# First cross attention: value tiles as the weights of the product, two heads in the array's column halves, normalised once per batch

## The chip, the cores and the metric

The kernel runs on one core of one Trainium2 chip. The time is that of one execution in device microseconds. Before the change three runs took 1884.75 to 1885.35 us, with a median of 1885.31 us; one more execution was profiled and took 1884.2 us, of which 1882.5 us are the span of its instructions. The core's engines are TensorE (PE in the profile, its weight loads PEld), VectorE (DVE), ScalarE (ACT), GpSimd (POOL) and SyncE (SP), which issues the DMAs. Each works through its own queue in order and waits on semaphores.

## What is computed

A stack of two layers. The change concerns the first step of the first layer, a cross attention with 16 batches, 64 queries per batch, 1601 keys, 16 heads of 32 columns:

```python
def _L0_xattn_ref(q, k, v, Wq, bq, Wk, bk, Wv, bv, Wo, bo):
    qh = (q @ Wq + bq).reshape(B, LQ, HEADS, D_K).transpose(0, 2, 1, 3)
    kh = (k @ Wk + bk).reshape(B, LKV, HEADS, D_K).transpose(0, 2, 1, 3)
    vh = (v @ Wv + bv).reshape(B, LKV, HEADS, D_K).transpose(0, 2, 1, 3)
    scores = jnp.einsum('bhqd,bhkd->bhqk', qh, kh) * scale
    attn = jax.nn.softmax(scores, axis=-1)
    out = jnp.einsum('bhqk,bhkd->bhqd', attn, vh)
    concat = out.transpose(0, 2, 1, 3).reshape(B, LQ, D_MODEL)
    return concat @ Wo + bo

x = x + _L0_xattn_ref(_layernorm(x), ctx_512, ctx_512, ...)   # x (16, 64, 512), ctx_512 (16, 1601, 256)
```

The rest (a state space layer, a blocked feed forward, a second cross attention, a self attention and a quantised feed forward) is as it was.

## The kernel before

`cross0` runs three blocks. `cross0_queries` makes the queries. `cross0_batches`, the one that matters here, makes the concatenated head outputs `catT`. `cross0_output` multiplies them by Wo. Float32 values are kept as two bfloat16 parts, a high part and the rest, and products are summed over the parts.

`cross0_batches` goes through 16 batches. A batch has 8 slots, one for each pair of heads (64 queries of one head in partitions 0 to 63, of the other in 64 to 127). While batch b is attended to, batch b+1's keys and values are projected. There are 29 projection groups per batch (`PROJ`): 16 for keys (six matmuls of 400 or 401 columns) and 13 for values (six of 512). `CUTS` deals them to the slots: four key groups in slots 0, 1, 3 and 5, three value groups in slots 2, 4 and 6, four value groups in slot 7. The last batch has none. The groups go through a ring of three PSUM banks.

In each slot the engines do, in the order of their queues:

- TensorE: the scores of the pair (24 matmuls in eight parts of the array, L552), the projection groups (L535), then the product of probabilities and values of the pair two slots back (L570). The scores need the exponential of the pair before (there is one buffer of scores); a group needs its ring bank free, which is when VectorE has taken the group three back.
- VectorE: the row maximum (L711), then for each group the low part (L681 or L687), for the second group of a slot the high part too (L670 or L674), and the reciprocal of the row sums (L694). In slot 2 it also takes the transposed output of the batch before, adding the bias (L722, four operations).
- ScalarE: two scalings of the product of the pair three slots back (L614, L615), the high part of the first group (L604 or L608), the exponential (L622), the high part of the third group, the high part of the probabilities (L632), the high part of the fourth group. When the exponential and L632 come is set by a count of the groups gone by: before the second and before the fourth event of the slot (the output counts as an event), or at the slot's end when there are fewer.
- GpSimd: the low part of the probabilities (L511), and the parts of the next context (L477, L484).
- SyncE: two transposing DMAs per pair (L451 high, L453 low), which bring the probabilities' parts to keys on partitions.

The product before has the transposed probabilities as weights (128 x 128) and 64 columns of values as the moving operand: high probabilities by high and low values, low probabilities by high values, 39 matmuls over 13 key tiles. Its four 32-column blocks hold two useful ones (each head's queries by its own values). L614 and L615 take these two into `o`, scaled by the reciprocal row sums. In slot 2 TensorE transposes `o` (L579, two transposes).

Of the kernel before, what the change touches and what calls it, by code (L numbers as in the profile page):

```python
# [314 lines left out]
EXP_AFTER = 1  # L315
NPT = len(PTILES)
# [44 lines left out]
def cross0_batches(k, ident, qT, wk, wv, bk, catT, bvT, wo):  # L361
    nc, d = k.nc, k.d
    with ExitStack() as ctx:
# [5 lines left out]
        v = k.sb(ctx, "x0_v", [P, 2, 2, NPT, D], BF16)  # L369
# [5 lines left out]
        rsum = k.sb(ctx, "x0_rowsum", [P, 4])  # L375
        rinv = k.sb(ctx, "x0_rowinv", [P, 4])
        o = spare[:, 2 * NKT:2 * NKT + 2 * NPAIR * DH].rearrange("p (u a d) -> p u a d", u=2, a=NPAIR)
# [25 lines left out]
        o_done = k.sem(ctx, "x0_o_done")  # L403
        wo_in = k.sem(ctx, "x0_wo_in")
        s_cat = k.sem(ctx, "x0_cat_done")
# [109 lines left out]
        def _(pe):  # L515
# [69 lines left out]
            for b, plan in enumerate(PLANS):  # L585
                for p in range(len(plan)):
                    if b < B:
                        scores_of(b, p)
                    for e, g, _ in ring_events(b, p):
# [4 lines left out]
                        else:  # L594
                            turned_out(e[1], g)

        @block.scalar
        def _(act):
            def project_hi(n, par, g):
# [18 lines left out]
            def exps(g):
                act.wait_ge(max_done, g + 1)
                if g >= 2:  # L620
# [3 lines left out]
                                     accum_out=rsum[:, g % 4:g % 4 + 1]).then_inc(exp_done, 1)  # L624
# [11 lines left out]
            for b, plan in enumerate(PLANS):  # L636
                for p in range(len(plan)):
                    pair = NPAIR * b + p
                    if 3 <= pair:
                        scaled(pair - 3)  # L640
                    todo = [exps, high] if b < B else []
                    seen = 0
                    for e, g, vector in ring_events(b, p):
# [7 lines left out]
                        if vector or e[0] == "out":  # L651
# [3 lines left out]
                    for do in todo:  # L655
                        do(pair)

        @block.vector
        def _(dve):
# [5 lines left out]
            def project_hi(n, par, g):  # L665
# [1667 lines left out]
```

## Time and profile before

| | us |
|---|---|
| median of three runs | 1885.31 |
| profiled execution | 1884.2 |
| its span | 1882.5 |

Of the span TensorE is busy 1635.2 us (87%), VectorE 1167.6 (62%), ScalarE 961.3 (51%), GpSimd 772.1 (41%). The first cross attention's batches run from about 100 to 895 us. In the page's row of slices TensorE shows 9 tenths or more there and the granted clock is full until the last batch. A timeline line gives start, duration, engine, source line, operation, output <- inputs, shape, count, and in brackets the idle time before it with what ended it. A matmul's duration in the list reaches past the start of the next one, so the pace is read from start to start. A slot is read from one row maximum on VectorE to the next. Some matmul records are missing, so a count can be short.

### The profile page before, as it was taken

To read this page: it belongs to the slowest core of one execution; us is meant where nothing else is said; L and a number is where in the kernel's file an instruction comes from. 1 tells how busy PE (TensorE), PEld (TensorE's weight loads), DVE (VectorE), ACT (ScalarE), POOL (GpSimd) and SP (SyncE) were. 2 spreads that over 40 slices of the span, in tenths; PEclk is the share of its full clock that TensorE was granted. 3 is DMA by queue.
4 is the path that set the end of the run, shared out by engine and by line. 5 is a ranking of instruction groups with operands and counts; after the bars stand their busy time and mean duration, and the time that the engine had idled before them with its cause. 6 is when DMAs were issued, how large, how long until landed. Compare 5 with 4: busy or idle time off the path is not lost. (4 is left out here: it accounts for less than half of the span.)

```text
span 1882.5 us, 36647 instructions
## 1 busy us (share of the span) xinstructions
PE 1635.2 (87%) x15032; PEld 888.8 (47%) x15144; DVE 1167.6 (62%) x1931; ACT 961.3 (51%) x1444; POOL 772.1 (41%) x379
## 2 busy tenths in 40 slices
PE   4799999999999999996889828989889989699449
PEld 2345555555555555554445413445434444344214
DVE  4477777877777787773555586779512221626891
ACT  1268888888888888875162323421102221227760
POOL 2257877777777787765000163532000000002410
PEclk9899999999999999995999868999999999799769
DMA  3459999999999999998300140234647944000001
GB/s 109 119 123 183 186 186 184 183 187 186 187 189 187 184 191 184 184 164 149 113 1 2 52 156 29 80 110 136 245 167 304 388 180 177 1 1 1 0 0 45
DMA packets 509506, 256.62 MB, mean 136 GB/s; under 512 B 443040, under 2 KB 490656, under 8 KB 506400
## 3 DMA queue, kind: packets, MB, share of 16 engines
q1 hardware_dynamic: 509344, 254.34, 58.4%
q8 instruction: 116, 1.90, 0.4%
q14 instruction: 46, 0.38, 0.1%
HBM read 130.29 MB, written 14.16 MB: 77 GB/s over the span
## 5 line engine op out<-in xcount | busy, mean ns | idle before, releaser
L511 POOL TENSOR_TENSOR x<-x_prob,x 128x1604 bf16<-128x1604 f32 x128 | 413.3, 3229 | 181.2 <-ACT x L632 180.9
L622 ACT ACTIVATE x_prob<-x_score,x_negmax 128x1604 f32<-128x1604 f32 x128 | 204.4, 1597 | 75.7 <-DVE x_negmax L711 74.7
L711 DVE TENSOR_REDUCE x_negmax<-x_score 128x1 f32<-128x1604 f32 x128 | 231.9, 1812 | 13.1 <-PE x_score L552 13.1
L681 DVE SCALAR_TENSOR_TENSOR x_kT<-x_ring,bk,x_kT 128x400 bf16<-128x400 f32 (+1 forms) x256 | 162.5, 635 | 118.3 <-ACT x_kT L604 115.6
L535 PE MATMUL x_ring<-x_ctx_hi,wk_split 128*128 128x400 bf16 (+1 forms) x1024 | 218.6, 335 | 11.6 <-POOL x_ctx_lo L484 9.3
L535 PE MATMUL x_ring<-wv_split,x_ctx_hi 128*128 128x512 bf16 (+1 forms) x770 | 200.3, 379 | 9.7 <-issue 9.6
L632 ACT CAST x<-x_prob 128x1604 bf16<-128x1604 f32 x128 | 195.9, 1531 | 0.3
L570 PEld LDWEIGHTS x_pv<-x_v,x_pT 128*128 128x128 bf16 (+1 forms) x4992 | 170.4, 100 | 42.5 <-ACT x L615 10.8
L570 PE MATMUL x_pv<-x_v,x_pT 128*128 128x64 bf16 (+1 forms) x4992 | 176.2, 196 | 14.0 <-DMA x_pT<-x 7.8
L687 DVE TENSOR_TENSOR x_v<-x_ring,x_v 128x512 bf16<-128x512 f32 (+1 forms) x208 | 143.2, 688 | 53.6 <-ACT x_v L608 51.5
L604 ACT ACTIVATE x_kT<-x_ring,bk 128x400 bf16<-128x400 f32 (+1 forms) x196 | 116.8, 596 | 76.8 <-PE x_ring L535 76.3
L535 PEld LDWEIGHTS x_ring<-x_ctx_hi,wk_split 128*128 128x128 bf16 x1024 | 92.1, 97 | 105.5 <-issue 16.5
L2009 PE MATMUL g_bank<-g_x_split,g_w 128*128 128x512 bf16 x564 | 126.1, 384 | 8.6 <-DVE g_x_split L2108 8.0
L535 PE MATMUL x_ring<-x_ctx_lo,wk_split 128*128 128x400 bf16 (+1 forms) x512 | 129.4, 334 | 0.0
L535 PEld LDWEIGHTS x_ring<-wv_split,x_ctx_hi 128*128 128x128 bf16 (+1 forms) x832 | 77.4, 99 | 102.3 <-issue 14.4
L535 PE MATMUL x_ring<-wv_split,x_ctx_lo 128*128 128x512 bf16 (+1 forms) x415 | 123.5, 379 | 0.1
L1975 POOL MEMSET g_round<- 128x1 f32 x1 | 0.1, 98 | 289.1 <-POOLq L1672 289.1
L484 POOL TENSOR_TENSOR x_ctx_lo<-x_stage,x_ctx_hi 128x802 bf16<-128x802 f32 (+1 forms) x64 | 106.4, 1663 | 15.9 <-DVE x_ctx_hi L663 14.6
L608 ACT CAST x_v<-x_ring 128x512 bf16<-128x512 f32 (+1 forms) x148 | 86.1, 582 | 52.3 <-PE x_ring L535 52.3
L2019 PE MATMUL g_bank<-g_wd,g_w 128*128 128x512 bf16 x282 | 63.6, 386 | 52.8 <-DVE g_w L2192 52.4
L1219 PE MATMUL f_bank<-f_x_split,f_w 128*128 128x512 bf16 x374 | 90.9, 392 | 12.7 <-POOL f_w L1106 12.1
L552 PE MATMUL x_score<-x_kT,x_q_rows 32*64 32x400 bf16 (+1 forms) x3072 | 94.7, 345 | 6.0 <-ACT x_prob L622 6.0
(313 smaller groups left out, 2539.2 us busy)
## 6 DMA issues: line engine op xcount, KB each, us to landing
y_ctx<-in_ctx SPq DMA_DIRECT2D x16, 1664.0 KB, 10.4
y_ctxT<-in_ctxT SPq DMA_DIRECT2D x16, 1601.0 KB, 14.0
x_stage<-in_ctxT SPq DMA_DIRECT2D x48, 400.0 KB, 4.5
x_q_rows<-q_rows SPq DMA_DIRECT2D x64, 128.0 KB, 3.3
f_split_stage<-in_L_ffn_w SPq DMA_DIRECT2D x8, 1024.0 KB, 5.2
x_stage<-in_ctxT SPq DMA_DIRECT2D x16, 401.0 KB, 4.8
x_pT<-x SPq DMA_TRANSPOSE x256, 4.5
f_split_stage<-in_L_ffn_w_up SPq DMA_DIRECT2D x12, 256.0 KB, 3.0
```

Source lines behind the costliest of these rows:

```text
L484: pool.tensor_tensor(clo[:, :, at], stage[:, c % 2, :, 0:n], chi[:, :, at], ALU.subtract).then_inc(clo_done, 1)
L511: pool.tensor_tensor(ph[:, g % 2, 1, 0:NKP], prob[:, g % 2, :], ph[:, g % 2, 0, 0:NKP], ALU.subtract).then_inc(pl_done, 1)
L535: last = pe.matmul(out_, lhs, rhs, start=(i == 0), stop=(i == len(steps) - 1))
L552: last = pe.matmul(score[L * u:L * u + L, 512 * c:512 * c + w], qp[rows, par, a, hq, p // 2, :], kT[rows, par, hk, p // 2, QW * c:QW * c + w],
L570: last = pe.matmul(pv[:, 0:2 * DH], pT[0:kw, u, hp, t, :], v[0:kw, vpar, hv, t, 2 * DH * pp:2 * DH * (pp + 1)], start=(hp == 0 and t == 0 ...
L604: nc.scalar.activation(kT[:, par, 0, m, n0:n0 + w], ring[g % RING][:, 0:w], ACT.Identity, bias=bk[:, KD * turned(c) + m:KD * turned(c) + m ...
L622: nc.scalar.activation(prob[:, g % 2, :].rearrange("p (c n) -> p c n", n=QW), scores, ACT.Exp, bias=nmax[:, g % 2:g % 2 + 1], accum_out=rs ...
L632: nc.scalar.copy(ph[:, g % 2, 0, 0:NKP], prob[:, g % 2, :]).then_inc(ph_done, 1)
L681: dve.scalar_tensor_tensor(kT[:, par, 1, m, n0:n0 + w], ring[g % RING][:, 0:w], bk[:, KD * turned(c) + m:KD * turned(c) + m + 1], kT[:, pa ...
L687: dve.tensor_tensor(v[0:kw, par, 1, m, :], ring[g % RING][0:kw, :], v[0:kw, par, 0, m, :], ALU.subtract).then_inc(ring_free, 1)
L711: dve.tensor_reduce(nmax[:, pair % 2:pair % 2 + 1], scores, mybir.AxisListType.XY, ALU.max, negate=True).then_inc(max_done, 1)
L2009: last = pe.matmul(banks[2 + n % NB_G][:], wt[:, hw, j, m * P:(m + 1) * P], xs[:, hx, j, 512 * c:512 * c + 512], start=(i == 0 and j == 0) ...
```

## The change

The operands of the product change places. The values are stored by head with the high and the low part beside one another (`v`, 64 columns for each head), and these 64 columns are the weights. The moving operand is 128 columns: 64 queries' high and 64 low probabilities of one head. The first head of a pair writes partitions 0 to 63 of the bank, the second 64 to 127, each in its half of the array's columns. That is 26 matmuls over the 13 key tiles. The result has rows (value part, value column) and columns (probability part, query), so both the columns' halves and the rows' halves must be added. VectorE adds the columns' halves for each pair (`summed`, a reduction of 128 values into 64, in place of ScalarE's two scalings). The rows' halves are added once per batch on TensorE (`folded`, replacing the two transposes): two float32 products with a folding matrix, and sixteen that spread the reciprocal row sums over the rows of the output. Then ScalarE copies these shares from PSUM (in slot 2's place of the output), VectorE multiplies the folded sums by them into `catT`, and ScalarE adds the bias at the head of slot 3 (`biased`, four operations). The product now waits for both transposes before its first matmul, and for `sum_done` in place of `o_done`.

```diff
@@ products @@
                 if g:
-                    pe.wait_ge(o_done, g)
+                    pe.wait_ge(sum_done, g)
                 pe.wait_ge(th_in[u], 16 * (g // 2 + 1))
-                for hp in range(2):
-                    if hp:
-                        pe.wait_ge(tl_in[u], 16 * (g // 2 + 1))
-                    for t, (k0, kw) in enumerate(PTILES):
-                        for hv in range(2 - hp):
-                            last = pe.matmul(pv[:, 0:2 * DH], pT[0:kw, u, hp, t, :],
-                                             v[0:kw, vpar, hv, t, 2 * DH * pp:2 * DH * (pp + 1)],
-                                             start=(hp == 0 and t == 0 and hv == 0), stop=(hp == 1 and t == NPT - 1))
+                pe.wait_ge(tl_in[u], 16 * (g // 2 + 1))
+                for t, (k0, kw) in enumerate(PTILES):
+                    for h in range(2):
+                        last = pe.matmul(pv[L * h:L * h + L, 0:2 * L],
+                                         v[0:kw, vpar, t, 2 * pp + h, :, :].rearrange("p s d -> p (s d)"),
+                                         pT[0:kw, u, :, t, L * h:L * h + L], start=(t == 0), stop=(t == NPT - 1))
                 last.then_inc(pv_done, 1)
 
-            def turned_out(b, g):
-                pe.wait_ge(o_done, NPAIR * (b + 1))
+            def folded(b, g):
+                if b == 0:
+                    pe.wait_ge(fold_set, 1)
+                pe.wait_ge(sum_done, NPAIR * (b + 1))
                 wait_bank(g)
-                for h in range(2):
-                    last = pe.transpose(ring[g % RING][:, P * h:P * h + P],
-                                        o[:, b % 2, 4 * h:4 * h + 4, :].rearrange("p a d -> p (a d)"), ident[:])
+                pe.wait_ge(inv_done, NPAIR * (b + 1))
+                for r in range(2):
+                    pe.matmul(ring[g % RING][L * r:L * r + L, 0:4 * L], fold[:].rearrange("p h d -> p (h d)"),
+                              sums[:, r::2, :], start=True, stop=True)
+                for n in range(4):
+                    for r in range(2):
+                        for h in range(2):
+                            pair = (NPAIR * b + 2 * n + r) % NINV
+                            rows = slice(L * r + DH * h, L * r + DH * h + DH)
+                            last = pe.matmul(ring[g % RING][rows, 4 * L + L * n:4 * L + L * n + L],
+                                             rinv[:, pair:pair + 1].broadcast_to([P, DH]), ident[:, L * h:L * h + L],
+                                             start=True, stop=True)
                 last.then_inc(ring_full, 1)
@@ ScalarE @@
-            def scaled(g):
-                pp, opar = g % NPAIR, g // NPAIR % 2
-                act.wait_ge(inv_done, g + 1)
-                act.wait_ge(pv_done, g + 1)
-                nc.scalar.activation(o[0:L, opar, pp, :], pv[0:L, 0:DH], ACT.Copy, scale=rinv[0:L, g % 4:g % 4 + 1])
-                nc.scalar.activation(o[L:P, opar, pp, :], pv[L:P, DH:2 * DH], ACT.Copy,
-                                     scale=rinv[L:P, g % 4:g % 4 + 1]).then_inc(o_done, 1)
+            def biased(b, g):
+                act.wait_ge(ring_free, g + 1)
+                for n in range(4):
+                    tile = catT[:, n, L * b:L * b + L]
+                    nc.scalar.activation(tile, tile, ACT.Identity, bias=bvT[:, n:n + 1])
...
-                    if 3 <= pair:
-                        scaled(pair - 3)
+                    while shifted:
+                        biased(*shifted.pop())
...
-                        if vector or e[0] == "out":
+                        if e[0] == "out":
+                            act.wait_ge(hi_done, g)
+                            act.wait_ge(ring_full, g + 1)
+                            nc.scalar.copy(shares, ring[g % RING][:, 4 * L:8 * L]).then_inc(hi_done, 1)
+                            shifted.append((e[1], g))
+                            continue
+                        if vector:
                             continue
@@ VectorE @@
             def inverse(g):
                 dve.wait_ge(exp_done, g + 1)
-                if g >= 4:
-                    dve.wait_ge(o_done, g - 3)
-                dve.reciprocal(rinv[:, g % 4:g % 4 + 1], rsum[:, g % 4:g % 4 + 1]).then_inc(inv_done, 1)
+                dve.reciprocal(rinv[:, g % NINV:g % NINV + 1], rsum[:, g % NINV:g % NINV + 1]).then_inc(inv_done, 1)
+
+            def summed(g):
+                dve.wait_ge(pv_done, g + 1)
+                dve.tensor_reduce(sums[:, g % NPAIR, :], pv[:, 0:2 * L].rearrange("p (s q) -> p q s", s=2), AX,
+                                  ALU.add).then_inc(sum_done, 1)
...
                         dve.tensor_reduce(nmax[:, pair % 2:pair % 2 + 1], scores, mybir.AxisListType.XY, ALU.max,
                                           negate=True).then_inc(max_done, 1)
+                    if 3 <= pair:
+                        summed(pair - 3)
...
                         elif e[0] == "out":
-                            dve.wait_ge(ring_full, g + 1)
-                            tok = slice(L * e[1], L * e[1] + L)
-                            for n in range(4):
-                                dve.tensor_scalar(catT[:, n // 2, n % 2, tok], ring[g % RING][:, L * n:L * n + L],
-                                                  bvT[:, n:n + 1], None, ALU.add).then_inc((hi_done, s_cat, s_cat, ring_free)[n], 1)
+                            dve.wait_ge(hi_done, g + 1)
+                            dve.tensor_tensor(catT[:, :, L * e[1]:L * e[1] + L],
+                                              ring[g % RING][:, 0:4 * L].rearrange("p (n q) -> p n q", n=4),
+                                              shares.rearrange("p (n q) -> p n q", n=4), ALU.mult).then_inc(ring_free, 1)
```

The tables `rsum` and `rinv` grow from 4 to 16 columns, the layouts of `v`, `catT`, the bias and Wo follow, and the writers of `v` write 32 columns at a time with a gap.

The order of the queues around the output. First ScalarE in a steady batch, slot 2 of batch 1 and the head of slot 3, before (x_prob is the probabilities, x their high part or, for L614 and L615, `o`):

```order
L608 CAST x_v<-x_ring 128x512
L622 ACTIVATE x_prob,x_rowsum<-x_score,x_negmax 128x1604
L608 CAST x_v<-x_ring 128x512
L632 CAST x<-x_prob 128x1604
L614 ACTIVATE x<-x_pv,x_rowinv 64x32
L615 ACTIVATE x<-x_pv,x_rowinv 64x32
L604 ACTIVATE x_kT<-x_ring,bk 128x400
```

and now (L667 is the copy of the shares, L635 the bias):

```order
L620 CAST x_v<-x_ring 128x16x32
L627 ACTIVATE x_prob,x_rowsum<-x_score,x_negmax 128x1604
L620 CAST x_v<-x_ring 128x16x32
L645 CAST x<-x_prob 128x1604
L667 COPY x<-x_ring 128x256
L635 ACTIVATE catT<-catT,bvT 128x64 x4
L616 ACTIVATE x_kT<-x_ring,bk 128x400
```

The copy stands behind the high part of the probabilities (L645), and the bias ahead of the next slot's first group. In the last batch there are no groups, and ScalarE's queue there now reads, slots 1 to 4:

```order
L627 ACTIVATE x_prob,x_rowsum<-x_score,x_negmax 128x1604
L645 CAST x<-x_prob 128x1604
L667 COPY x<-x_ring 128x256
L627 ACTIVATE x_prob,x_rowsum<-x_score,x_negmax 128x1604
L645 CAST x<-x_prob 128x1604
L635 ACTIVATE catT<-catT,bvT 128x64 x4
L627 ACTIVATE x_prob,x_rowsum<-x_score,x_negmax 128x1604
L645 CAST x<-x_prob 128x1604
L627 ACTIVATE x_prob,x_rowsum<-x_score,x_negmax 128x1604
```

Here the copy stands ahead of the slot's exponential. On TensorE the end of slot 2 of batch 1 reads now:

```order
L538 MATMUL x_ring<-wv_split,x_ctx_hi 128x512 x4
L538 MATMUL x_ring<-wv_split,x_ctx_lo 128x512 x2
L571 MATMUL x_pv<-x_pT,x_v 64x128 x26
L583 MATMUL x_ring<-x,x_fold 64x256 x2
L590 MATMUL x_ring<-ident,x_rowinv 32x64 x16
L555 MATMUL x_score<-x_kT,x_q_rows 64x401 x2
L555 MATMUL x_score<-x_kT,x_q_rows 64x400 x6
```

Eighteen matmuls stand where two transposes (L579) stood, between the product and the next scores.

## Rows read from the trace of the kernel before

**Rows 1.** Busy time by engine, 300 to 400 us (busy, instructions; clock, DMA, GB/s).

```profile
300.00:400.00 100.00, 98.60 (x1364) 58.74 (x1371) 78.51 (x118) 81.35 (x126) 78.71 (x34) 1.00 1.02 184
```

**Rows 2.** Timeline of DVE, one batch: start, us, operation, count [idle before, releaser].

```profile
395.24 1.83 DVE L711 TENSOR_REDUCE x_negmax<-x_score 128x1 f32<-128x1604 f32 x1 [0.32 <-PE x_score L552]
...
402.45 1.80 DVE L711 TENSOR_REDUCE x_negmax<-x_score 128x1 f32<-128x1604 f32 x1
...
409.04 1.81 DVE L711 TENSOR_REDUCE x_negmax<-x_score 128x1 f32<-128x1604 f32 x1
...
415.62 1.81 DVE L711 TENSOR_REDUCE x_negmax<-x_score 128x1 f32<-128x1604 f32 x1
...
419.66 0.69 DVE L687 TENSOR_TENSOR x_v<-x_ring,x_v 128x512 bf16<-128x512 f32 x1 [0.31 <-ACT x_v L608]
420.27 0.85 DVE L722 TENSOR_SCALAR catT<-x_ring,bvT 128x64 f32<-128x64 f32 x4
...
421.11 1.81 DVE L711 TENSOR_REDUCE x_negmax<-x_score 128x1 f32<-128x1604 f32 x1
...
427.69 1.81 DVE L711 TENSOR_REDUCE x_negmax<-x_score 128x1 f32<-128x1604 f32 x1
...
432.40 1.81 DVE L711 TENSOR_REDUCE x_negmax<-x_score 128x1 f32<-128x1604 f32 x1
...
438.99 1.81 DVE L711 TENSOR_REDUCE x_negmax<-x_score 128x1 f32<-128x1604 f32 x1
...
444.11 1.83 DVE L711 TENSOR_REDUCE x_negmax<-x_score 128x1 f32<-128x1604 f32 x1 [0.31 <-PE x_score L552]
```

**Rows 3.** Timeline of ACT, the same batch.

```profile
399.25 0.58 ACT L608 CAST x_v<-x_ring 128x512 bf16<-128x512 f32 x1 [0.29 <-PE x_ring L535]
...
404.29 1.60 ACT L622 ACTIVATE x_prob<-x_score,x_negmax 128x1604 f32<-128x1604 f32 x1 [0.23 <-DVE x_negmax L711]
...
406.36 1.52 ACT L632 CAST x<-x_prob 128x1604 bf16<-128x1604 f32 x1
407.78 0.60 ACT L604 ACTIVATE x_kT<-x_ring,bk 128x401 bf16<-128x401 f32 x1
```

**Rows 4.** Timeline of PE, the same batch.

```profile
399.00 1.03 PE L535 MATMUL x_ring<-wv_split,x_ctx_hi 128*68 128x512 bf16 x4
...
402.18 0.85 PE L535 MATMUL x_ring<-x_ctx_hi,wk_split 128*128 128x401 bf16 x4
...
406.27 1.31 PE L570 MATMUL x_pv<-x_v,x_pT 128*128 128x64 bf16 x39
407.50 0.72 PE L552 MATMUL x_score<-x_kT,x_q_rows 32*64 32x401 bf16 x24
408.15 0.85 PE L535 MATMUL x_ring<-x_ctx_hi,wk_split 128*128 128x400 bf16 x4
...
419.41 0.41 PE L579 MATMUL x_ring<-ident,x 128*128 128x128 f32 x2
```

**Rows 5.** Timeline of PE, later stages: products in column parts, float32 (two records each).

```profile
976.49 0.43 PE L940 MATMUL m_banks<-m_mix,m_xn 128*32 128x128 f32 x8 [1.79 <-DVE m_mix L1056]
...
1416.75 1.95 PE L1576 MATMUL y_pv<-y_ctx,y_pT 128*64 128x256 f32 x16 [0.24 <-ACT y_pT L1614]
...
1555.52 7.05 PE L1718 MATMUL s_bank<-s_xT,s_wq 128*64 128x512 f32 x16 [0.77 <-ACT s_xT L163]
```

**Rows 6.** Groups by shape, ACT, 90 to 900 us: busy and mean ns of one.

```profile
L608 ACT CAST x_v<-x_ring 128x512 bf16<-128x512 f32 x129 | 75.0, 582 | 49.5 <-PE x_ring L535 49.4
L615 ACT ACTIVATE x<-x_pv,x_rowinv 64x32 f32<-64x32 f32 x128 | 36.1, 282 | 1.6
```

**Rows 7.** Timeline of DVE, last batch.

```profile
847.17 1.83 DVE L711 TENSOR_REDUCE x_negmax<-x_score 128x1 f32<-128x1604 f32 x1 [1.16 <-PE x_score L552]
...
852.08 1.83 DVE L711 TENSOR_REDUCE x_negmax<-x_score 128x1 f32<-128x1604 f32 x1 [1.16 <-PE x_score L552]
...
877.95 1.83 DVE L711 TENSOR_REDUCE x_negmax<-x_score 128x1 f32<-128x1604 f32 x1 [1.53 <-PE x_score L552]
...
892.58 0.86 DVE L722 TENSOR_SCALAR catT<-x_ring,bvT 128x64 f32<-128x64 f32 x4 [10.89 <-PE x_ring L579]
```

**Rows 8.** Busy time by engine, 850 to 900 us (as rows 1).

```profile
850.00:900.00 50.00, 32.56 (x475) 22.00 (x473) 13.73 (x21) 25.94 (x39) 23.27 (x8) 0.60 0.88 166
```

**Rows 9.** Timeline of SP's queue, last transposing load.

```profile
886.39 1.48 SPq L453 DMA_TRANSPOSE x_pT<-x  x1
```

**Rows 10.** Timeline of PE, end of the stage.

```profile
890.25 0.88 PE L570 MATMUL x_pv<-x_v,x_pT 128*128 128x64 bf16 x13 [1.57 <-DMA x_pT<-x]
```

**Rows 11.** DMA issues of the page: operation, count, us to landing.

```profile
x_pT<-x SPq DMA_TRANSPOSE x256, 4.5
```

More of the change, by code:

```diff
@@ L315 @@
 EXP_AFTER = 1
+NINV = 16
 NPT = len(PTILES)
@@ L374, in cross0_batches @@
         nmax = k.sb(ctx, "x0_negmax", [P, 2])
-        rsum = k.sb(ctx, "x0_rowsum", [P, 4])
-        rinv = k.sb(ctx, "x0_rowinv", [P, 4])
-        o = spare[:, 2 * NKT:2 * NKT + 2 * NPAIR * DH].rearrange("p (u a d) -> p u a d", u=2, a=NPAIR)
+        rsum = k.sb(ctx, "x0_rowsum", [P, NINV])
+        rinv = k.sb(ctx, "x0_rowinv", [P, NINV])
+        sums = spare[:, 2 * NKT:2 * NKT + NPAIR * L].rearrange("p (a q) -> p a q", a=NPAIR)
+        shares = spare[:, 2 * NKT + NPAIR * L:2 * NKT + NPAIR * L + 4 * L]
+        fold = k.sb(ctx, "x0_fold", [P, 2, DH])
         zero = k.sb(ctx, "x0_zero", [P, KC])
@@ L402, in cross0_batches @@
         inv_done = k.sem(ctx, "x0_inv_done")
-        o_done = k.sem(ctx, "x0_o_done")
+        sum_done = k.sem(ctx, "x0_sum_done")
+        fold_set = k.sem(ctx, "x0_fold_set")
         wo_in = k.sem(ctx, "x0_wo_in")
-        s_cat = k.sem(ctx, "x0_cat_done")
         block = ctx.enter_context(nc.Block())
@@ L594, in _ @@
                         else:
-                            turned_out(e[1], g)
+                            folded(e[1], g)
         @block.scalar
@@ L607, in project_hi @@
                     kw = PTILES[m][1]
-                    nc.scalar.copy(v[0:kw, par, 0, m, :], ring[g % RING][0:kw, :]).then_inc(hi_done, 1)
-            def scaled(g):
-                pp, opar = g % NPAIR, g // NPAIR % 2
-                act.wait_ge(inv_done, g + 1)
-                act.wait_ge(pv_done, g + 1)
-                nc.scalar.activation(o[0:L, opar, pp, :], pv[0:L, 0:DH], ACT.Copy, scale=rinv[0:L, g % 4:g % 4 + 1])
-                nc.scalar.activation(o[L:P, opar, pp, :], pv[L:P, DH:2 * DH], ACT.Copy,
-                                     scale=rinv[L:P, g % 4:g % 4 + 1]).then_inc(o_done, 1)
+                    nc.scalar.copy(v[0:kw, par, m, :, 0, :],
+                                   ring[g % RING][0:kw, :].rearrange("p (h d) -> p h d", h=H)).then_inc(hi_done, 1)
             def exps(g):
@@ L656, in _ @@
                         do(pair)
+            biased(*shifted.pop())
         @block.vector
@@ L673, in project_hi @@
                     kw = PTILES[m][1]
-                    dve.tensor_copy(v[0:kw, par, 0, m, :], ring[g % RING][0:kw, :]).then_inc(hi_done, 1)
+                    dve.tensor_copy(v[0:kw, par, m, :, 0, :],
+                                    ring[g % RING][0:kw, :].rearrange("p (h d) -> p h d", h=H)).then_inc(hi_done, 1)
             def project_lo(n, par, g):
@@ L686, in project_lo @@
                     kw = PTILES[m][1]
-                    dve.tensor_tensor(v[0:kw, par, 1, m, :], ring[g % RING][0:kw, :], v[0:kw, par, 0, m, :],
-                                      ALU.subtract).then_inc(ring_free, 1)
+                    dve.tensor_tensor(v[0:kw, par, m, :, 1, :],
+                                      ring[g % RING][0:kw, :].rearrange("p (h d) -> p h d", h=H),
+                                      v[0:kw, par, m, :, 0, :], ALU.subtract).then_inc(ring_free, 1)
             def inverse(g):
                 dve.wait_ge(exp_done, g + 1)
-                if g >= 4:
-                    dve.wait_ge(o_done, g - 3)
-                dve.reciprocal(rinv[:, g % 4:g % 4 + 1], rsum[:, g % 4:g % 4 + 1]).then_inc(inv_done, 1)
+                dve.reciprocal(rinv[:, g % NINV:g % NINV + 1], rsum[:, g % NINV:g % NINV + 1]).then_inc(inv_done, 1)
[3 more added lines that the diff above has]
+                                  ALU.add).then_inc(sum_done, 1)
+            half = ident[:].rearrange("p (h s d) -> p h s d", h=2, s=2)
+            dve.tensor_tensor(fold[:], half[:, :, 0, :], half[:, :, 1, :], ALU.add).then_inc(fold_set, 1)
             for c in range(1, 4):
@@ L758, in _ @@
                 for i in range(4):
-                    last = pe.matmul(banks[t % NB_O][:], catT[:, i // 2, i % 2, t * P:(t + 1) * P], wo[:, i, :],
+                    last = pe.matmul(banks[t % NB_O][:], catT[:, i, t * P:(t + 1) * P], wo[:, i, :],
                                      start=(i == 0), stop=(i == 3))
@@ L2203, in cross0 @@
     with ExitStack() as c0:
-        catT = k.sb(c0, "catT", [P, 2, 2, TOK])
+        catT = k.sb(c0, "catT", [P, 4, TOK])
         bvT = k.sb(c0, "bvT", [P, 4])
@@ L2283, in lay_out @@
     f = np.ascontiguousarray
-    pairs = lambda a: a.reshape((2, 4, 2, DH) + a.shape[1:])
     ctx = i["ctx_512"]
@@ L2292, in lay_out @@
         "L0_xattn_bq": columns(i["L0_xattn_bq"]), "L0_xattn_bk": f(np.concatenate([np.roll(columns(i["L0_xattn_bk"]), ROWS * g, axis=0) for g in range(NROW)], axis=1)),
-        "L0_xattn_bv": f(pairs(i["L0_xattn_bv"]).transpose(1, 3, 0, 2).reshape(P, 4)),
-        "L0_xattn_Wo": f(pairs(i["L0_xattn_Wo"]).transpose(0, 2, 1, 3, 4).reshape(4, P, D)),
+        "L0_xattn_bv": columns(i["L0_xattn_bv"]),
+        "L0_xattn_Wo": f(i["L0_xattn_Wo"].reshape(4, P, D)),
         "L0_xattn_bo": f(i["L0_xattn_bo"].reshape(1, D)),
```

5 lines of the change are left out of this document (3 added, 2 removed).

## The prediction

> **What bounds the kernel now.** I read first the busy shares of the first cross attention, which fills about 100 to 895 us of the profiled execution. In its steady part TensorE is busy 98.6% at the full granted clock, ScalarE 81%, VectorE 79%, GpSimd 79% [rows 1]. By that view alone TensorE is the bound and every microsecond taken from it is won. The second view, the timeline of VectorE, says something else. Each slot (one pair of heads) begins on VectorE with the row maximum, so the starts of these reductions are the slots' lengths [rows 2]: 7.21 us for slot 7 of a batch (four value groups), 6.58 for each of the four slots with four key groups (402.45 to 409.04 to 415.62, 421.11 to 427.69, 432.40 to 438.99), 5.49 for slot 2 (three value groups and the output of the last batch), 4.71 for slot 4 and 5.12 for slot 6 (three value groups). A batch is 48.87 us (395.24 to 444.11). Only slot 7's reduction carries an idle time that ends with TensorE's scores, 0.32 us in one batch and 0.31 in the next. The others start because VectorE itself is through.
>
> ScalarE's timeline shows why [rows 3]. With R the start of the maximum, the exponential starts at R+1.84, the high part of the probabilities at R+3.91, the fourth group's high part at R+5.33, and VectorE's low part of that group and the reciprocal bring the next R at 6.58. Nothing of this key slot is TensorE's. A three-group slot closes already behind the third group, at 4.71. A four-value slot would need about 6.61 in the same way. So this chain of ScalarE and VectorE asks 4 x 6.58 + 2 x 4.71 + 5.49 + 6.61 = 47.8 us a batch.
>
> TensorE asks about as much [rows 4]: four key groups 4.09 us (402.18 to 406.27), so 1.02 each and 0.425 ns a column; a value group 1.02 x 512/401 = 1.30; the product with the values 1.23 (406.27 to 407.50); the scores 0.65 (407.50 to 408.15); the two transposes about 0.35 of the 0.41 shown. A batch: 16 x 1.02 + 13 x 1.30 + 8 x 1.88 + 0.35 = 48.6. The two chains are bound alternately, and what TensorE costs beyond the other one is 48.87 - 47.8 = 1.0 us a batch: 0.60 in slot 7, 0.41 in slot 6. That is all that a cheaper TensorE can win.
>
> **The change, TensorE.** Removed are 39 products of 64 columns (1.23 us). Added are 26 of 128 columns in alternating column halves. If halves overlap fully, 13 x 128 x 0.425 = 0.71 us; if not at all, 1.41. Later stages run float32 products in the same form, 128 rows and 64 columns [rows 5]: eight of 256 columns, alternating between the halves, take 1.95 us, 0.95 ns a column, while eight of 512 columns in one half take 7.05, 1.72 ns a column. Halves do overlap. I take 0.85, and keep 0.71 to 1.41. The fold adds two float32 products of 256 columns in two halves (0.49 by the first of these rates) and sixteen of 64 columns, 32 wide, in four column quarters. Four of that width and 128 columns took 0.43 [rows 5], so at most 4 x 0.43 = 1.7; streaming alone would be 0.4. I take 1.7 for the fold, keep 0.9 to 2.6 (all of them one behind the other, 1,536 columns at 1.72 ns). The new sum: 33.2 + 8 x (0.65 + 0.85) + 1.7 = 46.9 us a batch, below the other chain.
>
> The page "TensorE: Matmul & The Clock Gate" of the Trainium skill, section Back-to-back issue gap, gives about 81 ns for each matmul of 128 columns in a sustained stream with its weight load. That would be 2.1 us for the 26 products, more than is removed. "TensorEngine Tiling (Array Packing)" of the Trainium skill, Gotcha 2, adds that column tiling excludes the fast weight load. The trace has no bfloat16 pair of this shape; its float32 one overlaps, which is why I do not follow these rules for the forecast.
>
> **The change, VectorE.** Each slot gets one reduction of 128 values per row behind the maximum. The maximum reads 1604 in 1.81; small operations of 64 columns cost 0.21 each (four in 0.85), so I take 0.25, within 0.2 to 0.35. It lies where VectorE waits for ScalarE later in the slot: 0.31 us before the last low part of a three-group slot [rows 2], more in the others. It costs nothing up to 0.31, and 0.04 in three slots at 0.35.
>
> **The change, ScalarE.** The two scalings leave (0.28 us each [rows 6]). They stand at the head of a slot, where ScalarE has slack before the maximum ends, so they return nothing. In slot 2 there is a new step on the chain. Now VectorE reaches the output right after the third low part. In the changed order ScalarE does the third high part, then the 1.52 us high copy of the probabilities, and only then copies the 128 x 256 shares out of PSUM; VectorE multiplies after that. ScalarE is free at R+5.33. The copy is between 0.28 (32 columns) and 0.58 (512) [rows 6], I take 0.43; the multiplication 0.42 (0.69 for 512 less 256 at 1.04 ns); 0.03 more for reciprocal and hand-overs. Slot 2 becomes 6.20 instead of 5.49: +0.71. The fold must be full by R+5.33: the groups end near R+2.4, the product at 3.25, the fold at 4.95, and 0.25 later the reader starts (the group ended 399.00, ScalarE took it at 399.25). It just fits; a fold of 2.6 us would add 0.8. In slot 3 four bias operations, 0.3 each, come before the first high part; they end near R+1.2, that part takes 0.5 of ScalarE, and the exponential is still due at R+1.84. They are hidden by 0.1 us.
>
> **The steady sum.** Slot 6 returns to 4.71: -0.41. In slot 7 TensorE starts its scores only after the exponential of slot 6 (R+3.6), is through with three value groups at slot 7's R+3.4, and ScalarE can take the third at R+3.66 instead of R+3.43: the slot is 6.84, -0.37. With +0.71 in slot 2: -0.07 a batch. Fourteen batches give -1.0; the first batch has no output: -0.8. Together -1.8 us, with -8 (copy and multiplication at their least, slot 7 whole) to +12 (fold at 2.6) around it.
>
> **The end of the stage.** In the last batch no projections cover anything. Nominal slots are 4.91 [rows 7], the five to 877.95 average 5.17, and the clock's mean is 0.60 [rows 8]: the lower level, 1.2 GHz, most of the time. Here I count the new product as 1.5 us and the fold as 2.6.
> - In slot 2 the shares' copy now stands ahead of the exponential in ScalarE's queue, because no group pulls the exponential forward. The low transpose is issued at R+8.44 (877.95 to 886.39 [rows 7, 9]) and lands 3.9 (890.25, [rows 10]) to 4.5 us later [rows 11]. So the product of two slots back starts at R+2.5 to 3, ends near 4.2, the fold near 6.8, the copy near 7.3: the exponential starts some 5.3 us after R+1.84, and all of the chain behind it. About 1.3 us of present waits for transposes are absorbed.
> - The product now waits for both transposes before its first instruction: of today's 0.88 us after the last landing [rows 10] it makes 1.5. Where the transpose is last, three slots carry 0.6 more: 0.2 a slot, 1.2 in six.
> - After the last landing today 3.2 us remain (890.25 to 892.58 + 0.86 [rows 7, 10]). New: 1.5 + 0.25 + 2.6 + 0.43 + 0.42 + four bias operations 1.1 + hand-overs 0.3 = 6.6: +3.4 (at full clock 5.1, +1.9).
>
> Sum: 5.3 - 1.3 + 1.2 + 3.4 = +8.6 us, within 4 and 12. With the steady part: 8.6 - 1.8 = +6.8. The profiled execution was 1884.2 us (span 1882.5); its median of three 1885.3. Forecast: 1891.0 on the profiled one, 1892.1 for the median.
>
> **Rivals.**
> - *Small end.* The last batch overlaps more than I count (full clock, fold 1.3 us): +4 there, -4 in the steady part. 1885.5, no change. For it: both parts have such lower ends. Against: the queue order of ScalarE in the last batch is fixed.
> - *TensorE is the bound after all.* For it: 98.6% busy. Then a batch follows its sum, 46.9 instead of 48.87, 15 x -2.0 = -29.5, +8.6 at the end: 1864. It decides if key slots fall below 6.58. Against: four slots a batch show no wait for TensorE. It also holds, in a weaker form (down to about 1880), if slots 2 and 7 come shorter.
> - *Halves do not overlap in bfloat16* (weight loads of 64 columns in the open). Product 1.41, fold 2.6: 33.2 + 5.2 + 11.3 + 2.6 = 52.3 a batch, +3.4 x 15 = 51, with the end about 1945. It decides from a product of 1.05 us. (By the 81 ns of the Trainium skill's page above the product would be 2.1 us and the time near 2030.)
>
> **Chances.** Forecast 0.64, small end 0.16, TensorE bound 0.12, no overlap 0.08. The range 1884 to 1903 leaves the last two out; the forecast's own is 1888 to 1898. About 0.2%, 3.8 us, is what a measurement here tells from no change. Faster by more 0.12, within 0.17, slower 0.71.
>
> **What the next profile would show.** Product groups start to start 0.8 to 0.9; TensorE's steady busy share down by one or two points with waits on the exponential and on ring banks; key slots still 6.58; slot 2 near 6.2 with the shares' copy behind the high copy; slot 6 at 4.71; one slot of 10 us in the last batch. I am wrong if key slots change, if the product is above 1.05, or if the batch is not 48.8.

## The result and the profile after

The changed kernel takes 1890.38 us in the median of 14 runs, against 1885.09 us of the kernel before in the same session: a ratio of 1.0025, 95% interval 1.0014 to 1.0037. It is slower by 0.25%, 5.3 us. Its profiled execution has a span of 1889.2 us, 6.7 more than before. The last operation on `catT` ends at 900.23 us instead of 893.44, 6.8 later, and what follows takes 989.0 us in both profiles. So in these two executions all of the difference lies in this stage.

Busy time of the changed kernel, a steady stretch and the last batch (busy us and instructions of PE, PEld, DVE, ACT, POOL; granted clock, DMA share, GB/s):

```profile
300.00:400.00 100.00, 96.33 (x1246) 51.31 (x1252) 80.04 (x126) 76.81 (x105) 78.85 (x35) 1.00 1.01 184
850.00:900.00 50.00, 23.13 (x424) 15.08 (x400) 14.86 (x23) 22.72 (x29) 22.55 (x7) 0.52 0.72 129
```

TensorE has fallen from 98.6% to 96.3% and ScalarE from 81 to 77 [rows 1]. Both got work taken away, and a batch got only 0.06 us shorter.

VectorE's timeline, one batch (start, duration, operation; the row maxima are the slots, L718 is the sum of the columns' halves, L749 the multiplication by the shares):

```profile
394.37 1.81 DVE L738 TENSOR_REDUCE x_negmax<-x_score 128x1 f32<-128x1604 f32 x1
...
401.24 1.80 DVE L738 TENSOR_REDUCE x_negmax<-x_score 128x1 f32<-128x1604 f32 x1
...
409.56 0.28 DVE L718 TENSOR_REDUCE x<-x_pv 128x64 f32<-128x128 f32 x1
...
414.42 1.81 DVE L738 TENSOR_REDUCE x_negmax<-x_score 128x1 f32<-128x1604 f32 x1
...
420.16 0.42 DVE L749 TENSOR_TENSOR catT<-x_ring,x 128x256 f32<-128x256 f32 x1 [1.01 <-ACT x L667]
...
420.57 1.81 DVE L738 TENSOR_REDUCE x_negmax<-x_score 128x1 f32<-128x1604 f32 x1
...
438.46 1.81 DVE L738 TENSOR_REDUCE x_negmax<-x_score 128x1 f32<-128x1604 f32 x1
...
443.18 1.81 DVE L738 TENSOR_REDUCE x_negmax<-x_score 128x1 f32<-128x1604 f32 x1
```

Slot by slot against [rows 2], the maxima left out included: slot 7 6.87 (7.21 before), the two key slots 6.59 and 6.59, slot 2 6.15 (5.49), slot 3 6.59, slot 4 4.72, slot 5 6.58, slot 6 4.72 (5.12). A batch is 48.81 us (48.87). The sum of the halves takes 0.28 us and 0.19 to 0.20 of VectorE's row, and no slot is longer for it.

TensorE, slots 0 to 2 of the next batch (L571 the product, L583 and L590 the fold, L555 the scores, L538 a group):

```profile
404.97 0.92 PE L571 MATMUL x_pv<-x_pT,x_v 128*64 128x128 bf16 x26
405.82 0.71 PE L555 MATMUL x_score<-x_kT,x_q_rows 32*64 32x401 bf16 x24
...
410.44 0.85 PE L538 MATMUL x_ring<-x_ctx_hi,wk_split 128*128 128x400 bf16 x4 [0.74 <-DVE x_kT L702]
...
417.80 0.60 PE L583 MATMUL x_ring<-x,x_fold 128*64 128x256 f32 x4
418.33 0.65 PE L590 MATMUL x_ring<-ident,x_rowinv 128*32 128x64 f32 x32
418.92 0.72 PE L555 MATMUL x_score<-x_kT,x_q_rows 32*64 32x401 bf16 x24
```

The product takes 0.85 us from start to start (404.97 to 405.82; 1.23 before) and the fold 1.12 (417.80 to 418.92). The saving turns into a wait: at 410.44 the fourth key group stands 0.74 us idle until VectorE frees its bank.

ScalarE around the output, slot 2 and the head of slot 3:

```profile
418.32 1.54 ACT L645 CAST x<-x_prob 128x1604 bf16<-128x1604 f32 x1
419.75 0.38 ACT L667 COPY x<-x_ring 128x256 f32<-128x256 f32 x1
420.62 1.07 ACT L635 ACTIVATE catT<-catT,bvT 128x64 f32<-128x64 f32 x4 [0.49 <-DVE catT L749]
...
422.42 1.60 ACT L627 ACTIVATE x_prob<-x_score,x_negmax 128x1604 f32<-128x1604 f32 x1 [0.25 <-DVE x_negmax L738]
```

The copy of the shares (0.38 us) starts at 419.75, right behind the high copy, while the fold had been ready since 418.92. VectorE had stood idle for 1.01 us until this copy let it multiply, at 420.16. The four bias operations end before the exponential is due, which still waits 0.25 us for the maximum.

The last batch on TensorE:

```profile
854.69 1.60 PE L571 MATMUL x_pv<-x_pT,x_v 128*64 128x128 bf16 x26 [4.00 <-DMA x_pT<-x]
856.05 1.09 PE L583 MATMUL x_ring<-x,x_fold 128*64 128x256 f32 x4
...
896.24 1.12 PE L583 MATMUL x_ring<-x,x_fold 128*64 128x256 f32 x4 [0.38 <-DVE x L718]
```

On ScalarE, in the last batch:

```profile
858.28 0.37 ACT L667 COPY x<-x_ring 128x256 f32<-128x256 f32 x1 [7.30 <-PE x_ring L590]
858.55 1.60 ACT L627 ACTIVATE x_prob<-x_score,x_negmax 128x1604 f32<-128x1604 f32 x1
...
899.17 1.06 ACT L635 ACTIVATE catT<-catT,bvT 128x64 f32<-128x64 f32 x4 [0.49 <-DVE catT L749]
```

On VectorE, in the last batch:

```profile
850.78 1.83 DVE L738 TENSOR_REDUCE x_negmax<-x_score 128x1 f32<-128x1604 f32 x1 [1.17 <-PE x_score L555]
...
861.60 1.83 DVE L738 TENSOR_REDUCE x_negmax<-x_score 128x1 f32<-128x1604 f32 x1 [1.16 <-PE x_score L555]
...
881.90 1.83 DVE L738 TENSOR_REDUCE x_negmax<-x_score 128x1 f32<-128x1604 f32 x1 [1.17 <-PE x_score L555]
```

One slot is 10.82 us (850.78 to 861.60): the product waits for its transposing load until 854.69, the fold follows at the lower clock (1.2 GHz: the mean granted clock is 0.50 from 850 to 862), ScalarE stands idle for 7.30 us until the fold lets it copy, and only then comes the exponential (858.55, R+7.77). The last row maximum stands at 881.90 instead of 877.95 [rows 7].

### The profile page after: what moved, and what is told of

Same layout as the page of the kernel before. It is cut to its first block and busy times, and to the rows that moved or that the text cites. A ratio compares the mean times of both kernels' runs of the same rounds, so it can differ in the third digit from the quotient of the medians.

```text
span 1889.2 us, 34092 instructions
## 1 busy us (share of the span) xinstructions
PE 1613.7 (85%) x13912; PEld 826.2 (44%) x14024; DVE 1182.6 (63%) x2012; ACT 922.8 (49%) x1268; POOL 773.2 (41%) x379
## 3 DMA queue, kind: packets, MB, share of 16 engines
q1 hardware_dynamic: 509344, 254.34, 56.9%
## 5 line engine op out<-in xcount | busy, mean ns | idle before, releaser
L538 PE MATMUL x_ring<-x_ctx_hi,wk_split 128*128 128x400 bf16 (+1 forms) x1024 | 218.5, 335 | 27.7 <-DVE x_kT L702 18.4
L538 PE MATMUL x_ring<-wv_split,x_ctx_hi 128*128 128x512 bf16 (+1 forms) x770 | 200.3, 379 | 9.7 <-issue 9.4
L645 ACT CAST x<-x_prob 128x1604 bf16<-128x1604 f32 x128 | 195.9, 1531 | 0.3
L571 PE MATMUL x_pv<-x_pT,x_v 128*64 128x128 bf16 (+1 forms) x3328 | 124.3, 228 | 27.7 <-DMA x_pT<-x 16.5
L538 PEld LDWEIGHTS x_ring<-x_ctx_hi,wk_split 128*128 128x128 bf16 x1024 | 89.6, 97 | 127.7 <-DVE x_kT L702 39.9
L571 PEld LDWEIGHTS x_pv<-x_pT,x_v 128*64 128x64 bf16 (+1 forms) x3328 | 102.7, 114 | 77.9 <-issue 50.7
L538 PE MATMUL x_ring<-x_ctx_lo,wk_split 128*128 128x400 bf16 (+1 forms) x512 | 129.2, 334 | 0.0
L538 PE MATMUL x_ring<-wv_split,x_ctx_lo 128*128 128x512 bf16 (+1 forms) x415 | 123.5, 379 | 0.1
L538 PEld LDWEIGHTS x_ring<-wv_split,x_ctx_hi 128*128 128x128 bf16 (+1 forms) x832 | 77.3, 99 | 102.3 <-issue 14.7
L487 POOL TENSOR_TENSOR x_ctx_lo<-x_stage,x_ctx_hi 128x802 bf16<-128x802 f32 (+1 forms) x64 | 106.4, 1664 | 16.7 <-DVE x_ctx_hi L683 15.4
L1247 PE MATMUL f_bank<-f_x_split,f_w 128*128 128x512 bf16 x374 | 91.1, 393 | 13.3 <-POOL f_w L1134 12.8
L555 PE MATMUL x_score<-x_kT,x_q_rows 32*64 32x400 bf16 (+1 forms) x3072 | 95.2, 347 | 4.9 <-ACT x_prob L627 3.8
```

Of the source, the lines that this page charges most:

```text
L487: pool.tensor_tensor(clo[:, :, at], stage[:, c % 2, :, 0:n], chi[:, :, at], ALU.subtract).then_inc(clo_done, 1)
L538: last = pe.matmul(out_, lhs, rhs, start=(i == 0), stop=(i == len(steps) - 1))
L571: last = pe.matmul(pv[L * h:L * h + L, 0:2 * L], v[0:kw, vpar, t, 2 * pp + h, :, :].rearrange("p s d -> p (s d)"), pT[0:kw, u, :, t, L * h ...
L645: nc.scalar.copy(ph[:, g % 2, 0, 0:NKP], prob[:, g % 2, :]).then_inc(ph_done, 1)
```

## The experiments

The medians, and three lengths from the profiles, in us (the kernel before ran beside them, with medians of 1885.9 beside e1 to e4 and 1886.0 beside e5 to e8). "Stage" is the time from the first row maximum to the end of the last operation on `catT`, "last batch" the part of it from the last batch's first row maximum on. The batch is the mean of the fourteen that have an output:

| kernel | median | ratio to before, 95% | stage | a batch, mean | last batch |
|---|---|---|---|---|---|
| before | 1885.1 | | 784.3 | 48.87 | 51.2 |
| changed | 1890.4 | 1.0014 to 1.0037 | 791.1 | 48.84 | 59.3 |
| e1 | 1870.7 | 0.9907 to 0.9946 | 772.3 | 48.16 | 50.0 |
| e2 | 1878.9 | 0.9945 to 0.9981 | 778.1 | 48.57 | 51.3 |
| e3 | 1876.6 | 0.9932 to 0.9969 | 777.1 | 48.06 | 59.0 |
| e4 | 1888.9 | 1.0002 to 1.0029 | 787.7 | 48.83 | 56.0 |
| e5 | 1876.5 | 0.9925 to 0.9962 | 774.2 | 48.00 | 56.9 |
| e6 | 1893.8 | 1.0032 to 1.0075 | 791.4 | 48.93 | 58.3 |
| e7 | 1934.0 | 1.0225 to 1.0266 | 832.4 | 51.31 | 64.0 |
| e8 | 1861.6 | 0.9848 to 0.9887 | 761.4 | 47.13 | 56.4 |

The stage is counted from its first row maximum because its start differs: it stands at 109.1 us in the profiles of before and changed and at 106.5 to 108.6 in those of e1 to e8, behind code that no edit touches. Ends of the stage can therefore not be compared across these profiles.

**e1: how much the product can give at all.**

```diff
-                    for t, (k0, kw) in enumerate(PTILES):
+                    for t, (k0, kw) in enumerate(PTILES[0:1]):
...
-                                             start=(hp == 0 and t == 0 and hv == 0), stop=(hp == 1 and t == NPT - 1))
+                                             start=(hp == 0 and t == 0 and hv == 0), stop=(hp == 1 and t == 0))
```

> The kernel before with its product of probabilities and values summed over one key tile of thirteen (3 matmuls instead of 39), so most of the product is left out. Theory (ScalarE and VectorE hold a batch at 47.8 us whatever TensorE does): slot 6 falls from 5.12 to 4.7, slot 7 from 7.21 to 6.6, the key slots stay at 6.58 and slot 2 at 5.5; a batch 47.8 instead of 48.87, 15 of them -16 us, and the last batch -2 more: about 1867. Rival (TensorE is the bound): the whole product comes back, about 1.15 us x 8 x 15 = -138 us, about 1747.

Busy time of e1, the steady stretch:

```profile
300.00:400.00 100.00, 84.61 (x818) 42.18 (x824) 79.72 (x119) 82.25 (x126) 80.17 (x34) 1.00 0.96 189
```

VectorE of e1, slots 0 and 7 and the starts behind them:

```profile
395.26 1.80 DVE L711 TENSOR_REDUCE x_negmax<-x_score 128x1 f32<-128x1604 f32 x1
...
401.84 1.81 DVE L711 TENSOR_REDUCE x_negmax<-x_score 128x1 f32<-128x1604 f32 x1
...
436.53 1.81 DVE L711 TENSOR_REDUCE x_negmax<-x_score 128x1 f32<-128x1604 f32 x1
...
443.40 1.80 DVE L711 TENSOR_REDUCE x_negmax<-x_score 128x1 f32<-128x1604 f32 x1
```

This kernel leaves 36 of the product's 39 matmuls out, so its output is not the attention. That takes TensorE from 98.6 to 84.6% busy and saves 15 us, not 138 (12.0 of them in the stage). Key slots are 6.58 and 6.59, slot 2 is 5.48. The rival is refuted. One size of the theory was off: slot 7 is 6.87 (436.53 to 443.40), as in the changed kernel, as its four value groups after late scores make it, by the sum in the prediction; a batch is 48.14, not 47.8. So the most that a cheaper TensorE could win was 0.73 us a batch, and not the 1.0 of the prediction.

**e2 and e3: the chain of ScalarE and VectorE shortened, before and after the change.** The same two lines go from both kernels:

```diff
-                        elif seen == EXP_AFTER + 2 and todo:
-                            todo.pop(0)(pair)
```

> The kernel before with ScalarE's high copy of the probabilities moved behind the fourth group's high part. Theory: the chain of ScalarE and VectorE shrinks in the four key slots and slot 7 from 6.58 to about 5.2, but TensorE then asks 48.6 us a batch, so only 0.3 a batch comes back: -4 us, about 1881, key slots near 6.0 and TensorE without idle time. Rival (only the ScalarE and VectorE chain counts): -1.4 x 5 x 15 = -100 us.

> The changed kernel with the same move. Theory: here TensorE asks only 47.0 us a batch (key slots 5.67, slots of three value groups 5.49, slot 2 6.51, slot 7 6.79), so a batch falls from 48.80 to 47.0 to 47.3: -22 to -27 us against the changed kernel, about 1865, and the same edit is worth some 20 us more here than in the kernel before. Rival (TensorE's saving is lost elsewhere, on the transposing loads or GpSimd): a batch stays above 48 and TensorE waits for x_pT; -5 us or less.

VectorE of e2, the first row maximum of a batch and that of the next:

```profile
396.41 1.83 DVE L709 TENSOR_REDUCE x_negmax<-x_score 128x1 f32<-128x1604 f32 x1 [0.40 <-PE x_score L552]
...
444.99 1.83 DVE L709 TENSOR_REDUCE x_negmax<-x_score 128x1 f32<-128x1604 f32 x1 [0.40 <-PE x_score L552]
```

In e2 nearly every maximum now waits 0.4 us for the scores, a batch is 48.58 us, which is TensorE's sum (48.6), and the time falls by 7 us where 4 were expected. The stage is 6.2 us shorter: 4.2 in the fourteen batches with an output, as expected, and 2.2 in the first batch, which the sum had left out; the last one is not shorter. In e3 the key slots are 5.68 as TensorE's sum has them, but the time fell by 14 us against the changed kernel, not by 22 to 27. The direction is right, the size was not, and the rival named beside it came in part: the mean batch stays at 48.06 instead of 47.0 to 47.3. ScalarE of e3, slot 2 and the head of slot 3:

```profile
411.21 0.37 ACT L665 COPY x<-x_ring 128x256 f32<-128x256 f32 x1 [1.31 <-PE x_ring L590]
411.48 1.53 ACT L645 CAST x<-x_prob 128x1604 bf16<-128x1604 f32 x1
...
414.35 1.59 ACT L627 ACTIVATE x_prob<-x_score,x_negmax 128x1604 f32<-128x1604 f32 x1
```

The copy waits 1.31 us for the fold, with the high copy (411.48), the bias and the next exponential (414.35) queued behind it: slots 2 and 3 are 6.72 and 5.91 instead of 6.51 and 5.67, 6.3 us in fourteen batches. A second loss is in slots 5 and 6, which are up to 1.6 us too long in some batches, 8.4 us in all. TensorE's waits of e3 for these loads, 150 to 820 us (us in total, times, longest):

```profile
PE x_pv L571 <- DMA x_pT<-x: 7.6, 12, 1.5
```

And the same of the changed kernel:

```profile
PE x_pv L571 <- DMA x_pT<-x: 0.5, 1, 0.5
```

The transposing loads are now sometimes last.

**e4 and e5: the last batch.** In e4, in the last batch alone, ScalarE does exponential and high copy ahead of the copy of the shares; e5 is e3 with this:

```diff
                         if e[0] == "out":
+                            while b == B - 1 and todo:
+                                todo.pop(0)(pair)
                             act.wait_ge(hi_done, g)
```

> The changed kernel; in the last batch alone ScalarE does exponential and high copy before the copy of the shares. Theory: the slot of 10.82 us falls to 8.3, not to 5, because VectorE's multiplication by the shares still stands ahead of the next row maximum in its queue (copy at R+7.5, multiplication to R+8.3): -2.5 us, about 1888. Rival (the queue order of ScalarE is all of it): slot at 5.2, -5.5 us.

> The changed kernel with the high copy behind the fourth group's high part and, in the last batch alone, exponential and high copy ahead of the copy of the shares. The two gains lie in different places: -14 us and -2 to -3 against the changed kernel, about 1873. Rival (the last batch hides one of them): 1876.

The slot of the output in e4, two lines of TensorE and two of VectorE:

```profile
850.88 1.60 PE L571 MATMUL x_pv<-x_pT,x_v 128*64 128x128 bf16 x26 [2.79 <-DMA x_pT<-x]
...
854.28 1.23 PE L555 MATMUL x_score<-x_kT,x_q_rows 32*64 32x401 bf16 x24
...
854.88 0.42 DVE L751 TENSOR_TENSOR catT<-x_ring,x 128x256 f32<-128x256 f32 x1 [4.68 <-ACT x L669]
...
855.58 1.83 DVE L740 TENSOR_REDUCE x_negmax<-x_score 128x1 f32<-128x1604 f32 x1 [0.21 <-PE x_score L555]
```

The slot that began at 848.17 is 7.41 us instead of 10.82, between the 8.3 of the theory and the 5.2 of the rival. The theory's reason is not what the rows show: behind VectorE's multiplication (854.88) the row maximum still waits 0.21 us for the scores, and these stand in TensorE's queue behind the fold and a product that waited 2.79 us for its load. So it is the late load and the fold on TensorE that keep this slot long. The last batch is 3.2 us shorter than in the changed kernel. The median fell by only 1.5, and e5's not at all against e3 (its last batch is 2.1 us shorter). These are sizes that the medians do not resolve: e4's profiled execution had a span of 1896.0 us with 1001.6 of it after the stage, 12.6 more than the changed kernel's, in code that is the same. So the gain is shown for the last batch, not for the whole time.

**e6: the copy before the high copy, nothing else.**

```diff
-                        elif seen == EXP_AFTER + 2 and todo:
+                        elif seen == EXP_AFTER + 2 and todo and e[0] != "out":
```

> The changed kernel with one step moved: in the output's slot the copy of the shares stands ahead of the high copy, all else in the old order. Theory: VectorE is through with the slot at R+5.5 instead of 6.15, but ScalarE then still has 1.4 us of high copy, 1.1 of bias and 0.5 of a group before the next exponential, which starts at R+8.05 as against 7.99 now: what slot 2 gives, slot 3 takes, 0 to +1 us. Rival (the place of the copy on the chain is what the change loses): -0.65 x 14 = -9 us.

ScalarE of e6, slot 2 and the next slot's exponential:

```profile
418.17 0.37 ACT L667 COPY x<-x_ring 128x256 f32<-128x256 f32 x1 [0.69 <-PE x_ring L590]
418.44 1.53 ACT L645 CAST x<-x_prob 128x1604 bf16<-128x1604 f32 x1
...
421.31 1.59 ACT L627 ACTIVATE x_prob<-x_score,x_negmax 128x1604 f32<-128x1604 f32 x1
```

Slot 2 is 5.51 and slot 3 7.05, together 12.56 against 12.74: as said, slot 3 takes what slot 2 gives, and the rival's 9 us did not come. Slots 6 and 7 are longer in some batches, where TensorE waited for late transposing loads (eight times, 4.1 us in all, from 150 to 820 us; once, 0.5 us, in the changed kernel). The time is 3.4 us above the changed kernel's, where 0 to 1 was expected. The stage is only 0.3 us longer, so where the rest of these 3.4 us lies is open; the two intervals overlap.

**e7: one column half at a time.**

```diff
-                for t, (k0, kw) in enumerate(PTILES):
-                    for h in range(2):
+                for h in range(2):
+                    for t, (k0, kw) in enumerate(PTILES):
```

> The changed kernel with the product's loops exchanged: all 13 tiles of the first head in one column half, then all 13 of the second, same matmuls and weights. Theory (the halves overlap in time, which makes the 26 products 0.85 us): without it 26 x 54.4 ns = 1.41 us or a little more, TensorE asks 47.0 + 8 x 0.56 = 51.5 us a batch and becomes the bound: +2.7 x 15 = +40 us, and some +4 in the last batch at the lower clock, about 1935. Rival (the 0.85 us come from fewer weight loads, not from overlap): start to start stays 0.85 us and the time 1890.

TensorE of e7, one product and the scores behind it:

```profile
419.19 1.45 PE L571 MATMUL x_pv<-x_pT,x_v 128*64 128x128 bf16 x26
420.57 0.71 PE L555 MATMUL x_score<-x_kT,x_q_rows 32*64 32x401 bf16 x24
```

The same 26 matmuls take 1.38 us (419.19 to 420.57), a batch 51.3, and the time is 1934.0. With the same matmuls and weights, only the alternation differs: so the halves do overlap in the changed kernel, and the order of two loops is worth 44 us.

**e8: the version that beats both.** e3, and at the output, in every batch, what is left to do for the pair comes first:

```diff
                         if e[0] == "out":
+                            while todo:
+                                todo.pop(0)(pair)
                             act.wait_ge(hi_done, g)
```

> As the one before it, but in every batch the high copy of the output's slot stands ahead of the copy of the shares. Theory: with the copy first, ScalarE idles for the fold and does the high copy late, which makes slots 2 and 3 of 6.72 and 5.91 us where TensorE asks 6.51 and 5.67; with the high copy first both fall to that, -0.45 x 14 = -6 us: about 1867. Rival (the copy then stands late again, as in the changed kernel, R+6.15, and VectorE's next slot with it): slot 3 gets longer by what slot 2 gets shorter, 1873.

Busy time of e8, the steady stretch:

```profile
300.00:400.00 100.00, 98.22 (x1285) 53.77 (x1293) 85.96 (x133) 80.22 (x106) 81.35 (x35) 1.00 1.05 194
```

VectorE of e8, slots 2 and 3, and slot 2 of the next batch:

```profile
399.31 1.83 DVE L738 TENSOR_REDUCE x_negmax<-x_score 128x1 f32<-128x1604 f32 x1
...
406.06 1.81 DVE L738 TENSOR_REDUCE x_negmax<-x_score 128x1 f32<-128x1604 f32 x1
...
411.49 1.83 DVE L738 TENSOR_REDUCE x_negmax<-x_score 128x1 f32<-128x1604 f32 x1
...
446.29 1.83 DVE L738 TENSOR_REDUCE x_negmax<-x_score 128x1 f32<-128x1604 f32 x1
```

Its waits for the transposing loads, 150 to 820 us:

```profile
PE x_pv L571 <- DMA x_pT<-x: 1.1, 4, 0.4
```

Slots 2 and 3 are 6.75 and 5.43, 12.18 together, which is TensorE's 6.51 + 5.67. This batch (399.31 to 446.29) is 46.98 us, TensorE's sum again (the mean is 47.13), and the waits for transposing loads fell from 7.6 to 1.1 us. 1861.6 us is 0.9868 of the kernel before (0.9848 to 0.9887). I had expected 6 us less than e5 and got 15. The stage is 12.8 us shorter than e5's: 6.3 of it are slots 2 and 3, as expected, and most of the rest slots 5 and 6, which were not in my sum. That the late high copy of slot 2 had delayed the loads of the next slots fits the waits that fell; no run moves the loads alone.

## Why the prediction was right

The forecast was 1892.1 us, slower; measured were 1890.4. For the profiled execution it said +6.8 and that is what the stage shows; but this sum is closer than its parts, since the steady part gained 0.5 us less than said and the last batch lost 0.5 less. By its own steps:

- *The bound.* Key slots stayed at 6.58 to 6.59, the product's saving came back nowhere but in slots 6 and 7. e1 shows it without the change's other parts. Of the waits that the prediction listed as signs, those on ring banks came (15.7 us from 150 to 820 us) and those on the exponential did not.
- *Steady sum.* Slot 6 4.72 (said 4.71), slot 7 6.87 (6.84), slot 2 6.15 (6.20), slots 3, 4, 5 unchanged. A batch -0.06 (said -0.07). The last batch's first row maximum stands at 840.98 instead of 842.29: -1.3 (said -1.8). One slot 7 in fifteen, with its neighbour, was 0.45 longer, behind a late transposing load.
- *Product 0.85 us* (said 0.85), with 0.09 more to enter from a full-width group. *Fold 1.12* (said 1.7): the term was too large, as sixteen narrow matmuls of 64 columns take 0.59, where I let each four cost as much as four of 128 columns. Nothing in the steady part hung on it.
- *The last batch.* From its start to its last row maximum +5.3 (said 5.3 - 1.3 + 1.2 = 5.2). Here too terms cancel. The exponential of slot 2 started at R+7.77 and not at R+7.14: the load landed some 5.2 us after its issue instead of 3.9 to 4.5, so the product began at R+3.91 instead of R+2.5 to 3, and a shorter fold gave part of that back. The slot is 5.6 us longer than before, and the later ones together 0.35 shorter. From the last row maximum to the stage's end it is 18.33 instead of 15.49, +2.8 (said 3.4; at a mean granted clock of 0.54 the fold took 2.1 instead of 2.6, from 896.24 to the copy at 898.30). Together +8.1 (said 8.6).
- *Rivals.* TensorE as the bound is refuted by e1, at 1870.7 instead of 1747. That the halves do not overlap is refuted by e7, which shows what it would have cost, 44 us. The Trainium skill's rule of about 81 ns for a matmul of 128 columns ("TensorE: Matmul & The Clock Gate", section Back-to-back issue gap) is not met here: 0.85 us for 26 are 33 ns each in alternating halves and 1.38 are 53 ns in one half. The small end (+4 in the last batch, -4 in the steady part) did not come: they were +8.1 and -1.3. ScalarE's queue order is 3.2 us of the 8.1: without it (e4) the last batch costs 4.9.

Where the gain went: the product gives back 0.38 us, 3.0 a batch. Entering it costs 0.09 each time and the fold 0.8 more than the transposes, 1.5 a batch. So TensorE asks 1.5 us less a batch. Only 0.7 of that shortens slots, 6 and 7, since ScalarE and VectorE hold the other six, and slot 2, where their chain got a step more, takes 0.7 back. With that chain shortened in both kernels (e2 and e8) the mean batch is 48.57 and 47.13: 1.4 us, with the first batch 21.7 over fifteen, of which the last batch takes 5.1 back. That leaves 16.7 in the stage; 17.3 us are between the two medians. Moving one copy in ScalarE's queue is worth 7 us alone, the change alone costs 5, both with the output's order set right give 24.

## What to carry to other kernels

An engine that is 98% busy need not be the bound. Take the starts of one operation per loop turn on each engine, and ask for each turn which wait ended last: here six turns in eight closed without TensorE. Where two chains are within 2% of one another, shortening one of them gives little (7 us in e2, less than nothing in the change) and both together more than the sum (24 in e8). And look at what a new step stands behind in its queue, in the last turn above all, where the cover is gone.

## What was not expected of the hardware

- A transposing load took 3.8 to 7.1 us from issue to landing in the changed kernel's steady part (median 4.4). A product that needs both loads at its first instruction waited for one in one steady slot:

```profile
588.08 0.92 PE L571 MATMUL x_pv<-x_pT,x_v 128*64 128x128 bf16 x26 [0.49 <-DMA x_pT<-x]
```

- Bfloat16 products with 64-column weights, 128 columns moving: 33 ns each when they alternate between the column halves, 53 in one half.
- The code after the stage is the same in all these kernels. It took 989.0 us in the changed kernel's profiled execution, 994.9 in e5's, 998.7 in e7's and 1001.6 in e4's. TensorE's mean granted clock over the first 166 us of it was 0.96 in the changed kernel's and 0.87 in e4's. What lets the clock fall in some executions is open.
